# The opening of the first FFN: x in four transfers, two of four tiles normalised on ScalarE, the first products reordered

## What is computed

```
x = x + 0.5 * ffn(layernorm(x))
ffn(h):  wq = w.astype(float8_e4m3fn)                 # for gate_w, up_w (256x768), down_w (768x256)
         gate = silu((h @ gate_wq) * gate_scale);  up = (h @ up_wq) * up_scale
         return ((gate * up) @ down_wq) * down_scale
x = x + attention(layernorm(x));   x = x + 0.5 * ffn(layernorm(x))
```

## Time and profile before

| | before |
|---|---|
| time, median of 3 runs (lowest to highest) | 187.33 (187.22 to 188.22) |
| span of the profiled execution | 187.8 |
| PE, DVE, ACT, POOL busy share of the span | 91%, 76%, 56%, 34% |
| PE busy in the first five of 40 slices, tenths | 6, 7, 4, 5, 9 |
| granted PE clock in slices 3 to 5 (9.4 to 23.5), tenths of full speed | 8, 5, 5 |
| mean granted clock over the span | 0.960 |

### The profile page before, as it was taken

How to read it: one execution, slowest core, us unless ns; L and a number is a source line. 1 busy time by engine, 2 the same in 40 slices (tenths; PEclk the granted TensorE clock), 3 DMA queues, 4 the chain that set the end, 5 groups by cost and what they waited for, 6 DMA issues and landing times.

```text
span 187.8 us, 3246 instructions
## 1 busy us (share of the span) xinstructions
PE 171.6 (91%) x1091; PEld 131.9 (70%) x1091; DVE 142.9 (76%) x302; ACT 104.5 (56%) x202; POOL 62.9 (34%) x68
## 2 busy tenths in 40 slices
PE   6745999899899999998999999999999999799992
PEld 2223867688878775866687777867677887588882
DVE  2899589999745486667796968878799899636664
ACT  3164199767208448584939576674926763224710
POOL 3535363353825210124161605215263915000000
PEclk9985599999999999999999999999999999889998
DMA  5898004403000000000000000000000000011002
...
DMA packets 6848, 8.41 MB, mean 45 GB/s; under 512 B 416, under 2 KB 5552, under 8 KB 6832
## 3 DMA queue, kind: packets, MB, share of 16 engines
...
...
## 4 chain that ended last, share of the span: by engine, by line
PE 36%; POOL 8%; DVE 7%; issue 5%; ACT 4%; POOLq 0%; DVEq 0%; ACTq 0%
PE bank L1017 12%; POOL grstd L326 6%; PE bank L1044 3%; PE bank L1121 3%; PE bank L1184 3%; PE bank L1141 3%; PE bank L1097 3%; PE bank L1070 2%; ACT fhi L451 2%; DVE rot L740 1%; PE bank L1134 1%; PE bank L1084 1%; PE bank L1081 1%; PE bank L1166 1%; DVE fuse L685 1%
## 5 line engine op out<-in xcount | busy, mean ns | idle before, releaser
L1017 PE MATMUL bank<-hh,gate_r 128*128 128x512 f32 x96 | 30.3, 436 | 4.7 <-DVE hh L669 2.3
L1017 PE MATMUL bank<-hh,up_r 128*128 128x512 f32 x96 | 28.0, 415 | 0.0
L398 ACT ACTIVATE gact<-bank,vec 128x512 f32<-128x512 f32 x24 | 16.4, 684 | 17.0 <-PE bank L1017 16.9
L1017 PEld LDWEIGHTS bank<-hh,gate_r 128*128 128x128 f32 x96 | 17.9, 202 | 11.2 <-issue 4.3
L1044 PE MATMUL bank<-down_r,fhi 128*128 128x256 f32 x96 | 25.1, 298 | 0.3 <-DVE flo L693 0.3
L326 POOL TENSOR_TENSOR grstd<-gve,neg_half 128x16 f32<-128x16 f32 x8 | 23.4, 2928 | 0.7
L1044 PE MATMUL bank<-down_r,flo 128*128 128x256 f32 x96 | 23.5, 282 | 0.0
L1017 PEld LDWEIGHTS bank<-hh,up_r 128*128 128x128 f32 x96 | 19.3, 201 | 4.7
L748 DVE TENSOR_TENSOR sc<-bank,msk 128x512 f32<-128x512 f32 x32 | 21.3, 682 | 0.7 <-PE bank L1121 0.7
L685 DVE SCALAR_TENSOR_TENSOR fuse<-bank,vec,gact 128x512 f32<-128x512 f32 x24 | 17.9, 744 | 3.8 <-PE bank L1017 3.6
L302 POOL TENSOR_SCALAR ve<-mv 128x1 f32<-128x1 f32 (+2 forms) x13 | 4.2, 321 | 49.1 <-DVE mv L630 49.1
...
## 6 DMA issues: line engine op xcount, KB each, us to landing
...
out<-xt SPq DMA_DIRECT2D x8, 128.0 KB, 1.7
...
```

What stands on the lines that cost most here:

```text
L398: nc.scalar.activation(gact[:, j % 2, :], pairs[j // (NG * NI)][j % 2][0][:, :], ACT.Silu, scale=gate_col[:, i:i + 1]).then_inc(silu_done, 1)
L1017: mm = pe.matmul(dst[:, :], wr[m][:, k * I + i * P:k * I + (i + 1) * P], half[:, k, g % NG, :], start=(k == 0 and half is hhi), stop=(k == ...
```

## The change

x's first four tiles come in four transfers instead of one, and the order of SP's list changes. Tiles 0, 2, 4 and 6 are normalised on ACT (`norm_act`) as `x * rstd + shift`, where `shift_rows` on DVE makes `shift = -mean * rstd` for four tiles. `rest_h(0, ...)` stands ahead of the work on pieces 2 and 3 on DVE, and `split_h(0, ...)` ahead of `to_half(2)` on ACT. The first product pair is written as `first_gate_up`, all `hhi` matmuls and then all `hlo` ones, and `gate_up(1)` stands ahead of `turn_h(1)`.

```
+            def load_x(n):
+                sp.dma_start(xt[:, n, :], x_dram[0][:, n, :]).then_inc(x_in[n], 16)
+
+            load_x(0)
             load_piece(0)
-            sp.dma_start(xt[:, 0:TH, :], x_dram[0]).then_inc(x_in[0], 16)
+            load_x(1)
+            load_x(2)
+            load_x(3)
             load_piece(1)
-            load_piece(2)
             sp.dma_start(msk[:, :], mask_t).then_inc(mask_in, 16)
...
+            load_piece(2)
+            load_piece(3)
+            sp.dma_start(xt[:, TH:NT, :], x_dram[1]).then_inc(x_in[TH], 16)
...
+            def norm_act(n):
+
+                act.wait_ge(shift_done, n // TH + 1)
+                if n >= TH:
+                    act.wait_ge(turned, n - TH + 1)
+                nc.scalar.activation(h[:, n % TH, :], xt[:, n, :], ACT.Identity, scale=rstd[:, n:n + 1],
+                                     bias=shift[:, n:n + 1]).then_inc(h_act, 1)
...
+            def shift_rows(g):
+
+                a, b = root_groups[g]
+                dve.wait_ge(rstd_done, g + 1)
+                dve.scalar_tensor_tensor(out=shift[:, a:b], in0=mv[:, a:b, 0], scalar=-1.0, in1=rstd[:, a:b],
+                                         op0=ALU.mult, op1=ALU.mult).then_inc(shift_done, 1)
...
+                    if g < NG and t % 2 == 0:
+                        pe.wait_ge(h_act, g * TH // 2 + t // 2 + 1)
+                    else:
+                        pe.wait_ge(h_done, normed_until(n0 + t))
...
+            def first_gate_up():
+
+                pe.wait_ge(hhi_done, KC)
+                for half in (hhi, hlo):
+                    if half is hlo:
+                        pe.wait_ge(hlo_done, KC)
+                    for m in ("gate", "up"):
+                        pe.wait_ge(w_ready, 1 if m == "gate" else PIECES_NEEDED[0])
+                        for k in range(KC):
+                            mm = pe.matmul(pairs[0][0][m == "up"][:, :], wr[m][:, k * I:k * I + P], half[:, k, 0, :],
+                                           start=(k == 0 and half is hhi), stop=(k == KC - 1 and half is hlo))
...
             turn_h(0)
-            gate_up(0)
+            first_gate_up()
+            gate_up(1)
             turn_h(1)
-            for j in range(1, 9):
+            for j in range(2, 9):
                 gate_up(j)
```

More of the change, by code:

```diff
@@ L78, in rests, with normed_until @@
     return n - on_pool, on_pool
+def normed_until(n):
+    return (n + 1) // 2 if n < NT else n + 1 - NT // 2
 def products_until(g, i):
@@ L140, in macaron @@
         rstd = sb("rstd", [P, 3 * NT])
+        shift = sb("shift", [P, NT])
         h = sb("h", [P, TH, C])
@@ L207, in macaron @@
         b_turned_y = [b_gn] * (NT - 2) + b_sc[::-1]
-        x_in = [sem(f"x_in{g}") for g in range(NG)]
+        x_in = [sem(f"x_in{n}") for n in range(TH + 1)]
         mask_in, rows_in, ds_in = sem("mask_in"), sem("rows_in"), sem("ds_in")
@@ L220, in macaron @@
             sem(n) for n in ("stats_done", "aggr_done", "ve_done", "rstd_done", "h_done", "turned"))
+        shift_done, h_act = sem("shift_done"), sem("h_act")
         hhi_done, hlo_done, gate_done, up_done, silu_done, fuse_done, fhi_done, flo_dve = (
@@ L269, in _ @@
                 sp.dma_start(rows[at:at + n, :], src.rearrange("(i p) -> i p", p=P)).then_inc(rows_in, 16)
-            sp.dma_start(xt[:, TH:NT, :], x_dram[1]).then_inc(x_in[1], 16)
-            for q in range(3, len(PIECES)):
+            load_piece(2)
+            load_piece(3)
+            sp.dma_start(xt[:, TH:NT, :], x_dram[1]).then_inc(x_in[TH], 16)
+            for q in range(4, len(PIECES)):
                 load_piece(q)
@@ L499, in _ @@
             to_weights(0)
+            norm_act(0)
+            norm_act(2)
             to_half(1)
             to_weights(1)
-            to_half(2)
             split_h(0, 0)
             split_h(0, 1)
+            to_half(2)
             to_weights(2)
+            silu(0)
             to_half(3)
             to_weights(3)
-            silu(0)
+            norm_act(4)
+            norm_act(6)
             silu(1)
@@ L619, in tile_stats @@
                 if n < NT:
-                    dve.wait_ge(x_in[n // TH], 16)
+                    dve.wait_ge(x_in[min(n, TH)], 16)
                 elif n < 2 * NT:
@@ L795, in add_proj @@
                 dve.tensor_tensor(x1[:, c, :], b_gn[:, C:2 * C], x1[:, c, :], ALU.add).then_inc(x2_done, 1)
+            tile_stats(0)
             grid_step(0)
@@ L800, in _ @@
             grid_add(0)
-            tile_stats(0)
             tile_stats(1)
@@ L809, in _ @@
             mean_var(3)
+            grid_clip(1)
+            grid_add(1)
             grid_step(2)
-            grid_clip(1)
+            shift_rows(0)
+            norm_tile(1)
+            norm_tile(3)
             grid_clip(2)
-            grid_add(1)
+            turned_vectors()
+            rest_h(0, 0)
             grid_add(2)
-            for n in range(0, 4):
-                norm_tile(n)
-            tile_stats(4)
-            turned_vectors()
-            mean_var(4)
+            rest_h(0, 1)
             grid_step(3)
-            tile_stats(5)
             grid_clip(3)
-            rest_h(0, 0)
             grid_add(3)
-            tile_stats(6)
-            mean_var(5)
-            tile_stats(7)
-            mean_var(6)
+            for n in range(4, 8):
+                tile_stats(n)
+            for n in range(4, 8):
+                mean_var(n)
+            fuse_up(0)
             grid_step(4)
-            mean_var(7)
-            rest_h(0, 1)
             grid_clip(4)
+            shift_rows(1)
+            norm_tile(5)
+            norm_tile(7)
+            grid_add(4)
             grid_step(5)
-            for n in range(4, 8):
-                norm_tile(n)
-            fuse_up(0)
+            fuse_up(1)
+            rest_h(1, 0)
+            rest_h(1, 1)
             grid_clip(5)
-            grid_add(4)
-            rest_h(1, 0)
-            fuse_up(1)
-            rest_h(1, 1)
             grid_add(5)
@@ L991, in turn_h @@
                 for t in range(TH):
-                    pe.wait_ge(h_done, n0 + t + 1)
+                    if g < NG and t % 2 == 0:
+                        pe.wait_ge(h_act, g * TH // 2 + t // 2 + 1)
+                    else:
+                        pe.wait_ge(h_done, normed_until(n0 + t))
                     for k in range(KC):
@@ L995, in turn_h @@
                     mm.then_inc(turned, 1)
+            def first_gate_up():
[8 more added lines that the diff above has]
+                                           start=(k == 0 and half is hhi), stop=(k == KC - 1 and half is hlo))
+                        if half is hlo:
+                            mm.then_inc(gate_done if m == "gate" else up_done, 1)
             def gate_up(j, parts=("gate", "up")):
@@ L1050, in turn_h2 @@
             def turn_h2(c):
-                pe.wait_ge(h_done, NT + c + 1)
+                pe.wait_ge(h_done, normed_until(NT + c))
                 if c == 0:
```

## The result

The changed kernel takes 190.55 us, median of 4 runs (188.94 to 190.78), and the kernel before, run beside it on the same chip, 187.78 (187.22 to 188.4). The ratio is 1.0131 with a 95% interval of 1.0083 to 1.0179: slower, by 1.6 to 3.4 us (the medians differ by 2.8). Of the runs in this document, those on record as slow are left out of medians, ratios and counts of executions: one of e3 (571.32 us), two of e6, one of e11, two of e12, and of the kernel before two of 34 and two of 29. The profiled execution has a span of 188.6 us and a mean granted clock of 0.973.

What follows compares the result with a forecast made beforehand. DVE was taken as full from 24.22 to 47.20, so the start of fuse_up(2), 27.30, decides. Terms of +0.05 or +0.7, less up to 0.7 for an early piece 2, summed to about 0: 187.3 us, range 185.3 to 188.5.

Steps and rivals of the forecast that it cites:

- Rival 2: DVE waits behind POOL between rest_h(1, 1) and fuse_up(2): +1.1 there; 188.3 to 189 with piece 2 late; chance 0.23.
- The x and weight transfers: Opening transfers on SP's queue: four statistics end near 6.2 instead of 7.1; piece 2 lands at 8.1, bound 9.9.
- up to 0.7 if piece 2 lands ahead of subtract(1): Deduction from the total if piece 2's transfer lands before 7.9, with shift_rows then at 8.1.
- The new chain to w_ready 4: Opening up to to_weights(3): gate_up(0) done at 15.0 instead of 19.56, gate_up(1) at 18.1 after 3.1 us of idle PE.
- Half clock from 18.1: PE at gate_up(1) and the transposes: assumed to run at half clock from 18.1, as before 22.64 in the old trace.
- From there to fuse_up(2): From gate_up(1) to fuse_up(2): rest_h(1, 1) ends at 25.0, fuse_up(2) starts at 27.35 or 28.4; sum +0.05 or +0.7.
- the worse of my two cases: Before fuse_up(2): rest_f(1) gets in ahead of grid_add(5), which ends at 28.45; fuse_up(2) at 28.4, sum +0.7.
- the better one: Before fuse_up(2): grid_add(5) goes next after the clip and ends at 27.4; fuse_up(2) at 27.35, sum +0.05.
- Gives 0.4 back: Behind fuse_up(2): subtract(5) has POOL out of its way and takes 0.95 instead of 1.37.
- Norms moved to ACT: Opening on DVE and ACT: 1 us of DVE work saved, but all ahead of 24, where DVE idles anyway.
- DVE is full behind it, so each microsecond at fuse_up(2) is one at the end: From fuse_up(2) on: every microsecond gained or lost there is one at gate_up(4) and one at the end.
- rival 3: Whole kernel: no measurable change, 186.4 to 188.2, the earlier gate_up(0) spent waiting for pieces 2 and 3; chance 0.44.

Runs made afterwards that it cites:

- e3: Changed kernel with three extra matmuls on zeros on PE between gate_up(3) and gate_up(4), where PE waits; 189.8 us, ratio to before 1.0085.
- e6: Changed kernel with grid_add(2) and grid_step(3) ahead of rest_h(0, 0) on DVE, clip and add of piece 5 left late; 187.14 us, ratio 0.995.
- e11: e9 with x's first four tiles in one transfer, piece 2 fourth in SP's queue and first statistics as before; 186.85 us, ratio 0.9946.
- e12: Changed kernel with grid_clip(5) ahead of group 1's rest_h pair, and turn_h(1) ahead of gate_up(1) on PE; 189.62 us, ratio 1.0104.
- e4: Kernel before with grid_clip(5) moved on DVE to between rest_h(1, 1) and grid_add(5); 189.16 us, ratio 1.0056.
- e8: e5 with all eight norm_tile on DVE, no shift_rows and no norm_act; 186.6 us, ratio 0.9934.
- e5: Changed kernel with piece 5's clip and add ahead of group 1's rest_h, grid_add(2) and grid_step(3) ahead of rest_h(0, 0); 186.97 us, ratio 0.9936.
- e9: e5 with shift_rows(0), norm_tile(1) and norm_tile(3) ahead of grid_step(2) on DVE; 186.04 us, ratio 0.9905.

## Why the prediction was wrong

I forecast no change, 187.3, and the kernel is slower by 1.3%, outside the range. Rival 2 had the right place, too low a chance and too low a price (188.3 to 189), and my range ended at 188.5, inside that price. By the prediction's steps:

- **The x and weight transfers: right.** Statistics end at 6.1 (6.2 forecast). The transfer of piece 2, issued at 5.38, lands 3.1 us later, at 8.5; I took 8.1 with an upper end of 9.9. In SP's queue and in the list of transfers with KB and us to landing:

```profile
5.38 0.40 SPq L268 DMA_DIRECT2D raw<-in_L_ffn_gate_w  x1
```

```profile
raw<-in_L_ffn_gate_w SPq DMA_DIRECT2D x1, 256.0 KB, 3.1
```

  That excludes the "up to 0.7 if piece 2 lands ahead of subtract(1)" which I had taken off the total, and DVE waited 1.71 us for it. "DMA: Bandwidth & Descriptors" of the Trainium skill, Anatomy of one DMA, gives 2.6 us for such a transfer, an estimate by its fit, which is for the GpSimd path and not for SyncE's queue; measured were 3.1. My own 0.35 for the second 128 KB was on no row; this transfer took 0.8 more than the 2.3 of a 128 KB one, the queue's share in which isn't shown.
- **The new chain to w_ready 4: right.** shift_rows at 8.9; norm_act 0.60 us (0.56 taken); hhi at 12.0 (11.8); gate_up(0) done at 14.7 (15.0); the step of piece 3 stretched to 1.12 beside subtract(2), as forecast; to_weights(3) at 18.3 (18.1); a PE wait of 3.7 (3.1).
- **Half clock from 18.1: right,** though it fell only at 16.3, where I had expected about 12, and rose at 23.2.
- **From there to fuse_up(2): this step failed.** The rest_h pair ended at 25.55 (25.0 forecast; gate_up(1) started 0.27 late, and 21.6 plus 1.56 is 23.15 and not the 22.95 that I wrote for the end of the transposes). After it came the worse of my two cases: clip behind rest_f(0), rest_f(1) in between, add behind rest_f(1). I had written this case down, at 28.4, and then weighed it evenly against the better one and against an early landing, and called the sum zero. The trace of before gave ground for one case only: in both of its encounters DVE and POOL take turns, one instruction each. subtract(1), norm_tile(0), subtract(2), norm_tile(1) is the one; rest_f(0), the add, rest_f(1) the other. With the clip ahead of the add, turn-taking gives rest_f(0), clip, rest_f(1), add. fuse_up(2) came at 28.89, the 28.4 of this case and the half microsecond by which the pair was late: 1.59 us lost in the profiles at the step that the sum had put at nothing.
- **"Gives 0.4 back": right, 1.37 to 0.94.** fuse_up(3) starts at 30.42 instead of 29.26, 1.16 late.
- **A missing term: the clock behind the new wait.** The sum priced gate_up(4)'s wait at its own length. Behind 2.45 us of idling the clock was at half speed for 3.4 us from 30.0. e3 puts this at 0.46%, about 0.9 us.
- **The base.** I set the sum on the span of 187.8 and on the median of 187.33 alike. But a time can't be below its own span: the median execution had a span of some 185.2, and the profiled one was 2.6 us longer than that, with more half speed (the table above). The 27.30 of fuse_up(2) belongs to such an execution. What the typical one had there wasn't recorded. An estimate from e4, which is before plus the late clip: its rest_f(0) ends at 24.38 + 1.29 = 25.67, and the add alone, with its 0.82, would have ended at 26.5, with fuse_up(2) at 26.4. Against that the change loses 2.5 us at fuse_up(2), not 1.59. How this, the clock, and the stretch at 162 that only one of the two profiles has share the gap between +0.8 (spans of the profiles) and +2.8 (runs) isn't shown.
- **Norms moved to ACT, worth nothing: right** (e8 against e5).
- **"DVE is full behind it, so each microsecond at fuse_up(2) is one at the end": right to within 1 us.** The table of starts has 114.3 to 115.9 between the two. In the profiles without a stretch of half speed behind fuse_up(2) the difference is what POOL's instructions cost DVE there.
- **Where the gain of gate_up(0), 4.9 us, went:** 3.7 into the wait for pieces 2 and 3, as rival 3 said. e5 and e9 show that 1.3 of that can be had back by an order on DVE.

"GPSIMD Engine Reference" of the Trainium skill, Specifications, names DVE instructions in a two-port mode or with two SBUF inputs as those that contend with GpSimd. The runs agree: clip 0.55 to 1.56, add 0.96 to 1.91, shift_rows 0.16 to 0.68, while rest_h and fuse_up kept their 0.68 and 0.74 in every kernel. I had quoted the rule for exactly these two instructions and didn't let it decide; which of the two cases it would be, though, no rule that I quoted says, only the trace's order of turns.
